# The normalisation that opens the quantised feed-forward, interleaved with the second context attention

## The reference, cut to what matters

```python
x = x + tanh(g_xattn[3]) * L3_xattn(layernorm(x), ctx, ctx, WQ, WK, WV)   # masked attention
x = x + tanh(g_ffn[3])   * L3_ffn(layernorm(x), w_gate, w_up, w_down)     # quantised

def L3_ffn(x, ...):
    x = act_qdq(x)               # scale = max|x| over the WHOLE tensor / 32767, round, times scale
    up = act_qdq(x @ deq(w_up).T)
    gate = act_qdq(x @ deq(w_gate).T)
    gate = act_qdq(gate * u16(sigmoid(gate)))
    o = act_qdq(gate * up)
    return o @ deq(w_down).T
```

## Time and profile before

| | |
|---|---|
| median of three runs | 2136.6 us |
| the three runs | 2136.13, 2136.6, 2140.9 us |
| span of the profiled execution, first to last instruction | 2138.9 us |
| PE busy in the span | 1902.3 us (89%) |
| DVE busy | 1670.6 us (78%) |
| ACT busy | 1295.8 us (61%) |
| POOL busy | 257.8 us (12%) |
| mean granted clock of TensorE | 0.946 |

### The profile page before, as it was taken

The page is one execution under the profiler, slowest core; times in us unless marked ns, Lnnn a source line. Parts: engine busy times, 40 slices in busy tenths (PEclk is TensorE's granted clock), DMA queues, the critical chain, the costliest instruction groups (busy, mean ns, idle before and its releaser), DMA issues. The chain is left out here.

```text
span 2138.9 us, 48262 instructions
## 1 busy us (share of the span) xinstructions
PE 1902.3 (89%) x17713; PEld 1448.2 (68%) x17713; DVE 1670.6 (78%) x4756; ACT 1295.8 (61%) x3167; POOL 257.8 (12%) x551
## 2 busy tenths in 40 slices
PE   6999999999969989999989796999999893799608
PEld 5777787787759988778767574677677672344208
DVE  6787787787758969999967696777776497787894
ACT  5777777777742228888856464555454366218744
POOL 1111111111101111111111142000000023000000
PEclk9999999999979999999989898999999997799859
DMA  5222221111125531111100012223222110002452
GB/s 153 54 66 61 54 57 41 44 46 46 44 85 216 227 126 32 32 32 32 29 1 1 16 55 77 97 82 109 93 84 83 54 56 11 0 0 105 185 182 79
DMA packets 123404, 152.38 MB, mean 71 GB/s; under 512 B 45818, under 2 KB 98595, under 8 KB 121123
## 3 DMA queue, kind: packets, MB, share of 16 engines
q1 hardware_dynamic: 119986, 147.71, 22.3%
q10 hardware_dynamic: 3184, 1.58, 0.3%
HBM read 110.19 MB, written 22.28 MB: 62 GB/s over the span
## 5 line engine op out<-in xcount | busy, mean ns | idle before, releaser
L1833 ACT ACTIVATE arena<-banks,b1c 128x512 f32<-128x512 f32 x192 | 131.3, 687 | 142.3 <-PE banks L1657 140.8
L1762 DVE TENSOR_TENSOR arena<-arena 128x512 f32<-128x512 f32 (+1 forms) x256 | 170.3, 687 | 52.1 <-ACT arena L1833 48.2
L624 ACT ACTIVATE arena<-banks,arena 128x128 f32<-128x128 f32 x512 | 180.7, 373 | 1.3 <-DVE arena L570 1.3
L1667 PEld LDWEIGHTS banks<-w2a,arena 128*128 128x128 f32 x1024 | 122.0, 192 | 19.8 <-issue 19.8
L496 PE MATMUL banks<-arena,wk 128*128 128x128 f32 x1024 | 132.7, 283 | 1.9 <-DVE arena L594 1.9
L876 PE MATMUL banks<-we,arena 128*128 128x128 f32 x1024 | 132.2, 286 | 1.6 <-DVE arena L947 0.2
L535 PE MATMUL banks<-wv,arena 128*128 128x512 f32 x256 | 132.3, 599 | 0.0
L496 PEld LDWEIGHTS banks<-arena,wk 128*128 128x128 f32 x1024 | 120.5, 193 | 13.2 <-issue 10.8
L876 PEld LDWEIGHTS banks<-we,arena 128*128 128x128 f32 x1024 | 123.4, 197 | 7.3 <-DVE arena L947 6.5
L1667 PE MATMUL banks<-w2a,arena 128*128 128x128 f32 x1024 | 124.7, 275 | 0.0
L541 PEld LDWEIGHTS banks<-konst,arena 128*128 128x128 f32 x512 | 59.3, 142 | 94.8 <-DVE arena L552 60.1
(11 more groups left out here) (253 smaller groups left out, 4975.0 us busy)
## 6 DMA issues: line engine op xcount, KB each, us to landing
arena<-coef_scratch SPq DMA_DIRECT2D x32, 2048.0 KB, 8.3
arena<-arena SPq DMA_DIRECT2D x256, 64.0 KB, 2.0
gated_scratch<-arena SPq DMA_DIRECT2D x16, 768.0 KB, 3.2
arena<-gated_scratch SPq DMA_DIRECT2D x16, 768.0 KB, 4.3
arena<-z1T_scratch SPq DMA_DIRECT2D x128, 64.0 KB, 2.4
arena<-in_ctx_turned SPq DMA_DIRECT2D x32, 256.0 KB, 2.8
arena<-in_ctx SPq DMA_DIRECT2D x64, 64.0 KB, 2.1
z1T_scratch<-arena SPq DMA_DIRECT2D x64, 64.0 KB, 1.6
```

What stands on the lines that cost most here:

```text
L624: act.activation(prob[:, o, c * P:(c + 1) * P], ps[:, SCORES + o, c * P:(c + 1) * P], ACT.Exp, bias=low[:, o, c:c + 1], accum_out=total[:, ...
L1667: mm = pe.matmul(ps[:, OUT + g.par, j * D:(j + 1) * D], hT[g.par][:, c, j * P:(j + 1) * P], w, start=c == 0, stop=c == CHUNKS2 - 1)
L1762: dve.tensor_tensor(by_tile, by_tile, wide_coef[g.par][rows, e], ALU.mult).then_inc(s["scaled"].sem, 1)
L1833: act.activation(hT[g.par][:, c, :], ps[:, HID + c % NHID, :], ACT.Gelu, bias=k.b1c[:, c:c + 1])\
```

## The change

`steps` becomes a generator that yields, after each step, how many steps are left. Every engine function yields from it. `flamingo` then runs the stages' generators one after another, and the table `EARLY` says, for stage 7, at how few steps left of stage 6 an engine begins to run one step of stage 7 after each further step of stage 6. For these three engines the start of stage 7 waits only for the end of stage 5's updates.

`normalise` is rewritten for that: its statistics wait for `x_updated` of the tile in stage 6, they use slot 1 of the small tiles and signals of their own, and the order of the parts is other. In the merged list VectorE's step s of stage 6 is followed by: the affine columns of group s-2, the maximum of group s-4, the statistics of group s-1, the group that this same step has just updated. This goes for s = 1 to 16, three further steps follow. GpSimd's step s is followed by 1/sqrt of group s-1 (s = 1 to 15), ScalarE's step s by the four activations of group s-3 (s = 3 to 15). TensorE and SyncE are unchanged. The holders of the raw and dequantised weights, `q_raw` and `q_deq`, swap towards the top of the arena. `unrolled` and an unused class go away.

```diff
 def steps(eng, n, lead, lag, body):
     for s in range(-lead, n + lag):
         body(lambda k: Tile(s + k, (s + k) % 2) if 0 <= s + k < n else None)
+        yield n + lag - 1 - s
...
+EARLY = {(7, "vector"): 16, (7, "gpsimd"): 15, (7, "scalar"): 13}
+
+def stage_start(eng, k, no, early):
+    if no > early:
+        eng.wait_ge(*k.front(no - early)["x_updated"].all(0))
...
+def stage_program(eng, k, no, name, part):
+    stage_start(eng, k, no, (no, name) in EARLY)
+    yield from part[name](eng)
...
     def gpsimd(pool):
         def normalise(at):
-            if g := at(2):
-                if g.has(1):
-                    pool.wait_ge(*s["shift"](g.back(1)))
-                p_front(pool, g)
-        steps(pool, G, 2, 0, normalise)
+            g = at(0)
+            pool.wait_ge(*s["q_aggr"](g))
+            if g.has(1):
+                pool.wait_ge(*s["shift"](g.back(1)))
+            pool.tensor_scalar(k.ve[:, :, 1], k.mv[:, :, 1, 1], 1.0, EPS, ALU.mult, ALU.add)\
+                .then_inc(s["q_vareps"].sem, 1)
+            pool.wait_ge(*s["q_vareps"](g))
+            pool.tensor_tensor(k.rstd[:, :, 1], k.ve[:, :, 1], k.konst[:, C_MHALF:C_MHALF + GROUP], ALU.pow)\
+                .then_inc(s["q_rstd"].sem, 1)
+        yield from steps(pool, G, 0, 0, normalise)
...
     def vector(dve):
         def normalise(at):
-            if g := at(2):
-                if g.has(1):
-                    dve.wait_ge(*s["shift"](g.back(1)))
-                d_front.aggr(dve, g)
-            if b := at(0):
+            if g := at(1):
+                dve.wait_ge(*s["q_rstd"](g))
+                if g.has(2):
+                    dve.wait_ge(*s["xhs"](g.back(2)))
+                dve.tensor_copy(affine[:, g.par, 0, :], k.rstd[:, :, 1]).then_inc(s["shift"].sem, 1)
+                dve.scalar_tensor_tensor(out=affine[:, g.par, 1, :], in0=k.mv[:, :, 1, 0], scalar=-1.0, in1=k.rstd[:, :, 1],
+                                         op0=ALU.mult, op1=ALU.mult).then_inc(s["shift"].sem, 1)
+            if b := at(-1):
                 dve.wait_ge(*s["xhs"](b))
-                k.hold(dve)
-                dve.tensor_reduce(xmax[:, bass.ds(b.idx, 1)], xhs[:, b.idx, :], AX.X, ALU.max,
+                dve.tensor_reduce(xmax[:, b.idx:b.idx + 1], xhs[:, b.idx, :], AX.X, ALU.max,
                                   apply_absolute_value=True).then_inc(s["xmax"].sem, 1)
-            if new := at(3):
-                if g:
-                    dve.wait_ge(*f["aggr"](sub(g, GROUP - 1)))
+            if new := at(2):
                 for j in range(GROUP):
-                    d_front.stats(dve, new, j)
-            if g:
-                dve.wait_ge(*f["rstd_ready"](sub(g, GROUP - 1)))
-                dve.tensor_copy(affine[:, g.par, 0, :], k.rstd[:, :, 0]).then_inc(s["shift"].sem, 1)
...
-        steps(dve, G, 3, 0, normalise)
+                    dve.wait_ge(*f_before["x_updated"](sub(new, j)))
+                    dve.bn_stats(k.st[:, j, 1, :], k.x[:, sub(new, j).idx, :]).then_inc(s["q_stats"].sem, 1)
+                dve.wait_ge(*s["q_stats"](new))
+                for j in range(GROUP):
+                    dve.bn_aggr(k.mv[:, j, 1, :], k.st[:, j, 1, :]).then_inc(s["q_aggr"].sem, 1)
+        yield from steps(dve, G, 2, 1, normalise)
...
     def scalar(act):
         def normalise(at):
-            if g := at(1):
+            if g := at(0):
                 act.wait_ge(*s["shift"](g))
...
-        steps(act, G, 1, 0, normalise)
+        yield from steps(act, G, 0, 0, normalise)
...
         def run(engine, name):
+            programs = [stage_program(engine, k, no, name, part) if name in part else iter(())
+                        for no, part in enumerate(parts)]
+            for no, program in enumerate(programs):
+                beside = EARLY.get((no + 1, name), 0)
+                for left in program:
+                    if left < beside:
+                        next(programs[no + 1])
```

More of the change, by code:

```diff
@@ L453, in body @@
                 k.load_rest(sp, t.idx)
-        steps(sp, T, 3, 1, body)
+        yield from steps(sp, T, 3, 1, body)
     def gpsimd(pool):
@@ L749, in group_signals @@
     return f
[L752 to L808, removed]
@@ L866, in body @@
                 p_front(pool, g)
-        unrolled(G, 4, 0, body)
+        yield from steps(pool, G, 4, 0, body)
     def tensor(pe):
@@ L972, in body @@
                 weigh(nxt, 3, EXPERTS)
-        unrolled(G, 4, 1, body)
+        yield from steps(dve, G, 4, 1, body)
     def scalar(act):
@@ L1137, in body @@
                 weights_turned(t, 0)
-        steps(pe, T, 2, 2, body)
+        yield from steps(pe, T, 2, 2, body)
     def vector(dve):
@@ L1281, in body @@
                 p_front(pool, g)
-        steps(pool, G, 3, 0, body)
+        yield from steps(pool, G, 3, 0, body)
     folds = Folds(k)
@@ L1345, in body @@
                 update(g)
-        steps(dve, G, 3, 1, body)
+        yield from steps(dve, G, 3, 1, body)
     def scalar(act):
@@ L1996, in first @@
                 project(pe, g, s["p_psum"], freed, (1,))
-        steps(pe, G, 1, 0, first)
+        yield from steps(pe, G, 1, 0, first)
         scale_tensor(pe, "ug")
@@ L2004, in tensor @@
         pe.wait_ge(*s["pmax"].all(G))
-        steps(pe, G, 0, 0, second)
+        yield from steps(pe, G, 0, 0, second)
         scale_tensor(pe, "gs")
@@ L2061, in first @@
                 dve.tensor_scalar(xd[:, :], xq[:, :], scale["x"][:, :], None, ALU.mult).then_inc(s["xd"].sem, 1)
-        steps(dve, G, 2, 0, first)
+        yield from steps(dve, G, 2, 0, first)
         dve.wait_ge(*s["pmax"].all(G))
@@ L2078, in second @@
                     .then_inc(s["gsmax"].sem, 1)
-        steps(dve, G, 0, 0, second)
+        yield from steps(dve, G, 0, 0, second)
         dve.wait_ge(*s["gsmax"].all(G))
@@ L2133, in first @@
                 act.activation(xdT[:, g.idx, :], ps[:, 0, :], ACT.Copy).then_inc(s["xdT"].sem, 1)
-        steps(act, G, 1, 0, first)
+        yield from steps(act, G, 1, 0, first)
         scale_known(act, "ug")
@@ L2151, in second @@
                 act.activation(sig[g.par], gq[g.par], ACT.Sigmoid, scale=scale["ug"][:, 1:2]).then_inc(s["sig"].sem, 1)
-        steps(act, G, 0, 0, second)
+        yield from steps(act, G, 0, 0, second)
         scale_known(act, "gs")
```

84 lines of the change are left out of this document (35 added, 49 removed).

## The result

The changed kernel takes 2128.2 us in the median (2121.96 to 2129.22) against 2138.8 for the kernel before beside it; the ratio is 0.9939, with a 95% interval from 0.9925 to 0.9953. So it is faster, by 10 to 16 us. A second series gave 2125.5 us and 0.9945 (0.9926 to 0.9965). The profiled execution took 2127.76 us and has a span of 2126.0 us, 12.9 less than before. The forecast was 10.6 us less; the two medians lie 10.5 us apart in the first series and 14.0 in the second.

A forecast was written before the change was run, and what follows sets the result against it. VectorE was taken to bound stage 6, with GpSimd's latency beside it in the normalisation. Saved 35.15 us less added 18.33 and 6.25 gives 10.57; 2136.6 - 10.6 = 2126.0 us, range 2120.5 to 2133.

The forecast's parts named there:

- The bound: Stage 6 and normalisation: VectorE bounds stage 6, so moved work lengthens its steps; only latency and the last steps' spare go.
- The sum of 10.57 us: Net saving: 35.15 us saved after the last update, less 18.33 and 6.25 us added in stage 6.
- The step: VectorE's full step of stage 6: normalisation adds 2.02 us (1.88 to 2.36); s = 1 to 10 add 18.33 us.
- The last six steps: End of stage 6, s = 11 to 16: 22.10 us with the new work against 15.85, so 6.25 us more.
- The end: From the last update of `x` to the scale's reduction: 6.88 us remain of 42.03, saving 35.15 us.
- What hides the rest: Stage 6 queues: GpSimd's second power keeps at least 0.26 us of cover; ScalarE's added 1.65 us a step costs nothing.
- The added waits on `x_updated`: VectorE's statistics in stage 6: waits taken as nothing, at most 0.05 us a step, 0.8 us in all.
- The clock rival: Stage 6: waits drop TensorE's clock to 1.2 GHz and TensorE becomes the bound; 2141 to 2162 us, chance 0.07.
- What the sum had at zero: Projections after the normalisation: where the clock comes back may shift, 1.5 us either way, counted as zero.
- the latency around it and what the last steps of stage 6 have to spare: Normalisation and end of stage 6: the claimed source of the gain, since VectorE's work itself isn't hidden.

The follow-up runs named there:

- e3_hold: The changed kernel with the old normalisation's semaphore increments ahead of its aggregation and its maximum put back; ratio 0.9940 to the kernel before.
- e5_three_more: The changed kernel with three unread VectorE reductions more per group, for groups 0 to 12; ratio 1.0054 to the kernel before.
- e7_affine_pool: The changed kernel with the normalisation's two affine columns made by GpSimd instead of VectorE; ratio 0.9953 to the kernel before.

## Why the prediction was right

**The bound.** VectorE's list sets the pace of stage 6, before and after: that was the core, and the runs with one and three reductions more show it. The sum of 10.57 us stands against 12.49 measured in the stretch; the 1.9 us it lacks are 0.91, 0.31 and 0.70 in the three parts that follow. That the medians of the first series lie so near the forecast, 10.5 us apart, is partly luck: the parts outside the stretch, which the sum leaves at zero, differ by several us between profiles.

**The step.** 2.02 us forecast, 1.91 measured. The term that was too large is the one from statistics to aggregation: I took 1.00 us from a row in which a semaphore increment stands between the two, and the new list has none; it is 0.90, and 1.01 in the run that puts it back. In ten steps (s = 1 to s = 10) 17.42 us were added where I had 18.33, though step s = 8 has the idle 0.43 us, where I had foreseen none.

**The last six steps.** 6.25 us more forecast; measured 1812.58 - 1790.79 = 21.79 against 15.85, 5.94 more.

**The end.** 6.88 us forecast, 6.18 measured: the way over GpSimd took 1.79 and not 1.95 us, and from the copy over ScalarE to the last maximum 1.95 and not 2.47. The increments explain only a third of it. With them, in e3_hold, this end takes 6.41 us, and the last maximum begins 2.06 us after the copy:

```profile
1811.93 0.17 DVE L1972 COPY affine_of_norm<-rstd 128x4 f32<-128x4 f32 x1 [1.41 <-POOL rstd L1908]
...
1813.99 0.69 DVE L1978 TENSOR_REDUCE xmax<-arena 128x1 f32<-128x512 f32 x1 [0.64 <-ACT arena L2068]
```

The rewrite changed two more things on this way: the column of the maximum is a fixed slice and no longer `bass.ds(b.idx, 1)`, and GpSimd's pair has lost an increment of its own. No run puts either back, so the other 0.47 us stay open.

**What hides the rest.** No row of VectorE shows a wait on GpSimd in the full steps, and the cover of "at least 0.26" was 0.93 us. The added waits on `x_updated` cost nothing that can be seen: the statistics of the normalisation take 0.86 us for four, like the others.

**The clock rival.** It was given 0.07 and didn't come, but its first half does happen: the wait in each full step was 2.24 us (2.35 forecast), and in the run with the increments the clock fell after 2.35. In the changed kernel itself it fell in the last two steps of stage 6, where the output products again take 2.06 us:

```profile
1805.34 2.06 PE L1428 MATMUL banks<-arena 128*128 128x129 f32 x8 [0.61 <-DVE x_tiles L1447]
1808.77 2.06 PE L1428 MATMUL banks<-arena 128*128 128x129 f32 x8 [1.37 <-DVE x_tiles L1447]
```

VectorE's steps there are 3.44 and 3.43 us with no wait, so nothing was lost. The second half fails where I had put the limit: TensorE would need to be slow for more than half of its work. In e3_hold and e5_three_more it was slow for 3.4 us in two full steps and at full speed again before the next wait. The Trainium skill, "TensorE: Matmul & The Clock Gate", section "HAM oscillation — how this bites in real kernels", tells of the fall after waits between bursts. This case's traces agree with the fall and not with the loss, because here another engine sets the pace.

**What the sum had at zero.** Behind the scale the changed kernel is 3.4 us shorter, more than the 1.5 us I had allowed for the clock. All of it comes where the clock is low. The projections' start gains 0.5 us. Between the two passes of projections TensorE waits 1.2 and 0.7 us; before, its clock was low for the first matmuls after that, and in the changed kernel not:

```profile
1928.34 4.54 PE L1975 MATMUL banks<-arena,wup 128*128 128x512 f32 x6
```

```profile
1918.29 2.84 PE L1919 MATMUL banks<-arena,wup 128*128 128x512 f32 x6
```

The first row is of before, the second of after: the same six products, 1.7 us apart. Another 1.1 us come in the last stretch, where the clock returns 8.5 us after the last scale in place of 10.8. I can't call this an effect of the change. The three profiles without interleaving have the slow piece and take 310.1 to 310.6 us after the scale; ten of the eleven with it don't and take 305.2 to 307.3; the eleventh, e7_affine_pool, is interleaved and has it, at 310.0. What decides it stays open.

**What the reason was only half of.** I had said that what goes is "the latency around it and what the last steps of stage 6 have to spare", and gave no split. The run alone with a longer lead gives it: 9.3 us for the latency, with the old increments in it, and 3.2 us from running beside stage 6.

## What to carry to other kernels

Before work is moved beside another stage, look at which engine bounds each of the two: where it is the same one, the overlap saves only waits, and a longer lead in place may save most of them. Cost moved instructions by the distance between starts, and look at what stands between them, semaphore increments too. Where the bounding engine's list is full, the next gain is to hand part of it to an engine with room, in an order that keeps that engine's older customer first.

## What the runs showed of the hardware that was not expected

- A semaphore increment in VectorE's list that nobody waits for costs time: with 32 of them the stretch is 1.58 us longer, 0.05 us each on average, and the distance from the statistics to the aggregation goes from 0.90 to 1.01 us.
- TensorE's clock fell to 1.2 GHz after two waits of 2.35 us in steps of 6.92 us (e3_hold), but not after two of 2.34 us in the same run, not after 2.88 us in e7_affine_pool, and not in the full steps of the changed kernel, where the wait is 2.24 us in nearly every step and once 2.59. The wait alone doesn't tell when it falls; what does is open. Three waits of 4.0 us in the full steps of e5_three_more were each followed by a low piece, and the stage lost nothing.
- The part of the program up to the first statistics of stage 6 took from 1692 to 1705 us by profile, while the stretch repeated within 0.06 us.
